# Expert weights split ahead of the loop and streamed from device memory, instead of split on chip in each sequence

## The chip, the cores and the metric

The kernel runs on one core of a Trainium2 chip. The core has five engines with queues of their own: TensorE (PE in the rows, its weight loads PEld), VectorE (DVE), ScalarE (ACT), GpSimd (POOL) and SyncE (SP), which here only issues DMAs. They meet through semaphores. The metric is the device time of one launch in microseconds (us). The kernel before takes 3360.27 us, the median of 3 runs (3360.13 to 3360.79).

## The reference

Two transformer-like layers over x of shape 8 x 1024 x 128 (8 sequences of 1024 tokens, width 128), all in float32. Both layers do `x = x + attention(layernorm(x)) + experts(layernorm(x))`:

```python
x  = h_t                                   # (8, 1024, 128)
xn = layernorm(x)
x  = x + latent_attention(xn) + experts_top2(xn)     # layer 0: 8 heads of 128, softmax over 1024 keys
xn = layernorm(x)
x  = x + linear_attention(xn) + experts_top4(xn)     # layer 1: 16 heads of 8, sums over tokens, no softmax matrix

# both mixtures: 8 experts, inner width 256, evaluated densely and weighted per token
for e in range(8):
    g, u = xn @ w_gate[e].T, xn @ w_up[e].T          # 128 -> 256 each
    out += weight[:, e:e+1] * (act(g, u) @ w_down[e].T)   # layer 0: silu(g)*u; layer 1: clipped, with biases
```

The router of layer 0 keeps two experts (thresholded softmax weights), that of layer 1 four.

## The kernel before

The program loops over the 8 sequences (`BATCH`, `SEQ = 1024`). All weights lie in SBUF from the start. Tokens lie as columns in the transposed tiles `xT[0]` and `xT[1]` (128 x 1024), one for each layer.

**Order of the work.** Nothing schedules this program: each engine's function is written out by hand, and each step waits on named semaphores. In layer 0 the attention has steps `w`, 0 to 71: 4 query projections, 32 score tiles (8 token blocks by 4 heads), again 4 queries and 32 tiles. A tile is: scores on PE, row maximum on DVE (L823), exponential on ACT (L551), transposes on PE two steps later (L1202), copied out half by ACT (L539) and half by DVE (L831), then the value product (L1216) for each four tiles. `UNIT_STEP` is 74; the last steps of the attention run beside the first expert units.

**Experts.** A layer has 16 chunks `f` (8 experts, two halves of 128 of the inner width) and 32 units `u` (a chunk by one half of the tokens). `gate_up(u)` makes six matmuls of 128x512 (L1121): each operand is split in a high part, rounded to the fast float32r format, and a low part, the rest, and the product is high x high + high x low + low x high, for gate and for up. In layer 0 ACT takes silu (L581) and DVE the product (L891); in layer 1 DVE adds the biases and clips (`limits`, L928 and L932), ACT takes silu (L604), DVE multiplies (L1037). POOL then multiplies by the routing weight (L450), and PE does `down(u)` four units later (L1128). `gate_up(u)` of layer 1 waits for `limits(u - 2)`, since the PSUM banks are two deep. Beside the units of layer 1, `flow_step(u)` does the linear attention in pieces (L951, L955, L977 and others on DVE; L1294, L1301, L1318 and L1326 on PE).

**Splits.** The high and low parts are made in each sequence. For the tokens, ACT casts `xT[l]` into `x_high` (L522) and DVE subtracts it for `x_low` (L802), in layer 0 at the end of the attention. For the weights ACT casts chunk `f` (128 x 256, L529) and DVE subtracts (L807), 16 chunks a layer, into one of four slots of `w_split`. `x_high`, `x_low` and `w_split` are views of `q_parts`, which holds the split queries of the attention, so none of them can be filled before the last score tiles have been read.

**Routing weights.** The transposed weights `gate_wT` go out to device memory (L390) and come back as one broadcast row of 512 KB for each expert (L398), in four slots. The first row of a layer is waited for by POOL.

**Before the loop.** SP issues the loads (L374 to L378). When all are in, ACT scales `w_down[1]` (L476), PE and DVE fold the attention's projections together (L634 and L636, L1053 to L1068), then the first sequence is normed.

Of the kernel before, what the change touches and what calls it, by code (L numbers as in the profile page):

```python
# [7 lines left out]
F32 = mybir.dt.float32  # L8
# [5 lines left out]
P = 128  # L14
# [28 lines left out]
ROUTER_EXP_STEPS = (18, 20)  # L43
GATES_STEP = QUAD + NT * QUAD + 3
# [46 lines left out]
UNITS_EACH = FH * HALVES  # L91

# [44 lines left out]
def two_layer_kernel(nc, ins, out):  # L137
    with ExitStack() as ctx:
# [69 lines left out]
        gate_rows = nc.dram_tensor("gate_rows", (2, E, SEQ), F32, kind="Internal").ap()  # L208
        ffn_s = sb("ffn_s", [P, 3, BANK])
# [27 lines left out]
        w_gate_up = [sb(f"w_gate_up{l}", [P, E * FH, 2, P]) for l in range(2)]  # L237
# [33 lines left out]
        def banks(a, n=2):  # L271
# [40 lines left out]
        w_high_ready = signal("w_high_ready", 2 * E * FH)  # L312
        w_low_ready = signal("w_low_ready", 2 * E * FH)
# [45 lines left out]
            (w_gate_up[0][:, :, :, :], "gate_up0"), (w_down[0][:, :, :], "down0"),  # L359
            (w_router[0][:, :], "router0"), (w_qkv[:, :], "W_QKV"), (w_proj[:, :], "W_PROJ"),  # L360
            (w_gate_up[1][:, :, :, :], "gate_up1"), (w_down[1][:, :, :], "down1"),
# [10 lines left out]
        def _(sp):  # L372
            for dst, name in loads:
                sp.dma_start(dst, ins[name]).then_inc(weights_in.sem, 16)  # L374
            for dst, name, n in rows:

                sp.dma_start(dst[:, 0:n], ins[name].partition_broadcast(P)).then_inc(weights_in.sem, 16)
            sp.dma_start(x_in[:, :, :], ins["x"][0, :, :].rearrange("(n p) d -> p n d", p=P)  # L378
                         ).then_inc(x_loaded.sem, 16)
            sp.sem_inc(y_stored.sem, 1)  # L380
            with sp.Fori(0, BATCH) as index:
# [5 lines left out]
                for l in range(2):  # L387
# [4 lines left out]
                    for e in range(E):  # L392
# [80 lines left out]
        def _(act):  # L473

            act.wait_ge(weights_in.sem, ALL_WEIGHTS)
# [30 lines left out]
            make_keys_high(None)  # L506
            with act.Fori(0, BATCH) as index:
# [7 lines left out]
                def split_high(l):  # L515

                    if l == 0:

                        act.wait_ge(scores_ready.sem, scores_ready.at(b, TILES - 2))
                    else:  # L520
                        act.wait_ge(xT_ready.sem, xT_ready.at(b, 2))
                    nc.scalar.copy(x_high, xT[l][:, :]).then_inc(x_high_ready.sem, 1)  # L522
# [906 lines left out]
```

## Time and profile before

| | |
|---|---|
| median of 3 runs | 3360.27 us |
| the profiled execution's own time | 3356.34 us |
| its span | 3354.5 us |
| granted TensorE clock, mean | 0.96 of full speed |
| PE busy | 3010.1 us, 90% of the span |
| DVE busy | 2371.5 us, 71% |
| ACT busy | 1556.0 us, 46% |
| POOL busy | 764.2 us, 23% |
| DMA | 89.17 MB, mean 27 GB/s |

The rows of the trace are from this one profiled execution. A busy share is a mean over stages: the sequence from about 462 to 872 us on the time axis is looked at below, because the first one contains the preparation. PE's shares flatter it, since the ends of matmuls are modelled; the waits stand more surely in the rows than the busy time does.

### The profile page before, as it was taken

What the parts mean: (1) busy time and instruction counts of PE and PEld (TensorE: products, weight loads), DVE (VectorE), ACT (ScalarE), POOL (GpSimd) and SP (SyncE); (2) the same over time, 40 slices, a digit from 0 to 9 for tenths busy, and PEclk for the clock granted to TensorE, in tenths of its full rate; (3) what the DMA queues carried; (4) which work ended last, traced back from release to release, by engine and by line L of the source; (5) the groups of instructions that cost most, each with busy time, mean ns of one, the idle gap of its engine ahead of it and who ended that gap; (6) DMA issues with size and microseconds to landing.
All of it is one profiled execution on the core that took longest, in us unless ns stands there. A gap on an engine that the chain in (4) does not pass through costs nothing.

```text
span 3354.5 us, 66466 instructions
## 1 busy us (share of the span) xinstructions
PE 3010.1 (90%) x21792; PEld 2176.3 (65%) x21792; DVE 2371.5 (71%) x3881; ACT 1556.0 (46%) x2742; POOL 764.2 (23%) x566
## 2 busy tenths in 40 slices
PE   5999889997899888998889988899788998999978
PEld 3786567765677556775567755677566775567755
DVE  3775777658776587765977659776597765977658
ACT  2663246623466234652356523565225652366423
POOL 0004320043201441013410235002340032500324
PEclk8999899999999899999999989999899998999989
DMA  2000100001000010000100001000000000000000
GB/s 103 11 23 26 51 15 27 7 21 51 14 27 8 19 51 14 27 14 13 51 15 27 21 13 45 15 27 21 32 26 14 27 27 32 20 15 27 26 32 26
DMA packets 40191, 89.17 MB, mean 27 GB/s; under 512 B 4048, under 2 KB 22681, under 8 KB 39321
## 3 DMA queue, kind: packets, MB, share of 16 engines
q1 hardware_dynamic: 39832, 84.55, 7.4%
q8 instruction: 206, 3.38, 0.4%
q14 instruction: 153, 1.25, 0.1%
HBM read 79.82 MB, written 4.72 MB: 25 GB/s over the span
## 4 chain that ended last, share of the span: by engine, by line
PE 69%; DVE 13%; issue 10%; ACT 4%; POOL 2%; DMA 1%; DVEq 1%; ACTq 0%; POOLq 0%; SPq 0%
PE ps L1121 16%; PE ps L1183 14%; PE ps L1202 12%; PE ps L1128 8%; PE ps L1216 7%; PE ps L1235 3%; DVE ffn_g L928 2%; DVE ffn_gu L1037 2%; DVE probsT L951 1%; PE ps L1093 1%; DVE ffn_u L932 1%; PE ps L1230 1%; PE ps L1294 1%; PE ps L1148 1%; ACT q_parts L512 1%
## 5 line engine op out<-in xcount | busy, mean ns | idle before, releaser
L450 POOL TENSOR_TENSOR probs<-ffn_gu,gate_bc 128x512 f32<-128x512 f32 x416 | 560.0, 1348 | 2331.4 <-DVE ffn_gu L891 1805.5
L1121 PE MATMUL ps<-q_parts 128*128 128x512 f32 x3072 | 940.4, 442 | 110.2 <-DVE ffn_u L932 58.0
L1121 PEld LDWEIGHTS ps<-q_parts 128*128 128x128 f32 x3072 | 569.2, 190 | 429.7 <-issue 230.9
L823 DVE TENSOR_REDUCE neg_max<-ps 128x1 f32<-128x1024 f32 x512 | 625.6, 1222 | 224.9 <-PE ps L1183 220.1
L551 ACT ACTIVATE probs<-ps,neg_max 128x1024 f32<-128x1024 f32 x512 | 571.3, 1116 | 223.5 <-DVE neg_max L823 220.6
L1183 PE MATMUL ps<-keys,q_parts 128*128 128x512 f32 x2048 | 606.9, 419 | 27.8 <-ACT probs L551 16.2
L1202 PE MATMUL ps<-ident,probs 128*128 128x128 f32 x4096 | 540.5, 274 | 18.1 <-DVE probsT L831 12.8
L1202 PEld LDWEIGHTS ps<-ident,probs 128*128 128x128 f32 x4096 | 478.8, 141 | 103.9 <-DVE probsT L831 21.7
L1128 PE MATMUL ps<-probs,w_down 128*128 128x512 f32 x832 | 436.8, 612 | 45.6 <-POOL probs L450 44.8
L1183 PEld LDWEIGHTS ps<-keys,q_parts 128*128 128x128 f32 x2048 | 347.7, 189 | 133.4 <-issue 64.3
L539 ACT COPY probsT<-ps 128x512 f32<-128x512 f32 x512 | 297.9, 582 | 203.8 <-PE ps L1202 203.4
L604 ACT ACTIVATE ffn_s<-ffn_g 128x512 f32<-128x512 f32 x256 | 160.7, 630 | 491.6 <-DVE ffn_g L928 491.4
L891 DVE TENSOR_TENSOR ffn_gu<-ffn_s,ps 128x512 f32<-128x512 f32 x256 | 175.4, 685 | 275.5 <-POOL probs L450 131.1
L831 DVE COPY probsT<-ps 128x512 f32<-128x512 f32 x512 | 348.3, 680 | 11.6 <-PE ps L1202 11.6
L581 ACT ACTIVATE ffn_s<-ps 128x512 f32<-128x512 f32 x256 | 152.9, 597 | 385.2 <-PE ps L1121 385.2
L1216 PE MATMUL ps<-probsT,latent 128*32 128x128 f32 x8192 | 276.7, 276 | 13.2 <-DVE x_mid L856 13.2
L1216 PEld LDWEIGHTS ps<-probsT,latent 128*32 128x32 f32 x8192 | 208.0, 109 | 57.6 <-DVE x_mid L856 23.8
L1128 PEld LDWEIGHTS ps<-probs,w_down 128*128 128x128 f32 x832 | 158.6, 193 | 112.3 <-POOL probs L450 69.0
L928 DVE TENSOR_SCALAR ffn_g<-ps,b_gate 128x512 f32<-128x512 f32 x256 | 190.0, 742 | 15.6 <-PE ps L1121 10.0
L816 DVE SCALAR_TENSOR_TENSOR q_parts<-ps,b_q,q_parts 128x1024 fp32r<-128x1024 f32 x64 | 82.1, 1283 | 126.7 <-ACT q_parts L512 126.7
L1037 DVE SCALAR_TENSOR_TENSOR ffn_gu<-ffn_u,ffn_s 128x512 f32<-128x512 f32 x176 | 138.1, 788 | 35.7 <-ACT ffn_s L604 35.7
L450 POOL TENSOR_TENSOR ffn_h<-ffn_gu,gate_bc 128x512 f32<-128x512 f32 x96 | 124.9, 1301 | 156.3 <-DVE ffn_gu L1037 114.4
(169 smaller groups left out, 2741.8 us busy)
## 6 DMA issues: line engine op xcount, KB each, us to landing
gate_bc<-gate_rows SPq DMA_DIRECT2D x128, 512.0 KB, 3.8
x_in<-in_x SPq DMA_DIRECT2D x9, 512.0 KB, 3.8
w_gate_up<-in_gate_up SPq DMA_DIRECT2D x2, 2048.0 KB
out<-x_mid SPq DMA_DIRECT2D x8, 512.0 KB, 3.4
w_down<-in_down SPq DMA_DIRECT2D x2, 1024.0 KB
probsT<-in_W_O SPq DMA_DIRECT2D x1, 512.0 KB
gate_rows<-gate_wT SPq DMA_DIRECT2D x16, 32.0 KB
w_qkv<-in_W_QKV SPq DMA_DIRECT2D x1, 192.0 KB
```

The costliest lines, as they stand in the source:

```text
L450: nc.gpsimd.tensor_tensor(ffn_h[u % 5], ffn_gu[:, u % 3, :], gate_bc[:, e % GATE_SLOTS, c * BANK:(c + 1) * BANK], ALU.mult).then_inc(h_rea ...
L539: nc.scalar.copy(probsT[:, t % (2 * QUAD), 0:BANK], ps[:, 4, :]).then_inc(low_copied.sem, 1)
L551: nc.scalar.activation(probs[:, t % 3, :], banks(2 * (t % 2)), ACT.Exp, bias=neg_max[:, t % 4:t % 4 + 1], accum_out=row_sum[:, g % 2, t % ...
L823: nc.vector.tensor_reduce(neg_max[:, t % 4:t % 4 + 1], banks(2 * (t % 2)), X, ALU.max, negate=True).then_inc(max_ready.sem, 1)
L831: nc.vector.tensor_copy(probsT[:, t % (2 * QUAD), BANK:SEQ], ps[:, 5, :]).then_inc(high_copied.sem, 1)
L928: nc.vector.tensor_scalar(ffn_g[:, u % 3, :], ps[:, u % 2, :], b_gate[:, f:f + 1], LIMIT, ALU.add, ALU.min).then_inc(gate_lim.sem, 1)
L1037: nc.vector.scalar_tensor_tensor(ffn_gu[:, u % 3, :], ffn_u[u % 3], 1.0 - LIMIT, ffn_s[:, u % 3, :], ALU.max, ALU.mult).then_inc(gu_done.s ...
L1121: mm = nc.tensor.matmul(ps[:, bank, :], w_split[:, f % 4, h, k * P:(k + 1) * P], tokens[:, half], start=(part == 0), stop=(part == 2))
L1128: nc.tensor.matmul(ps[:, 4 + c, :], w_down[l][:, f, :], ffn_h[u % 5], start=(l == 0 and f == 0), stop=(f == E * FH - 1)).then_inc(down_don ...
L1183: mm = nc.tensor.matmul(ps[:, 2 * (t % 2) + c, :], q_parts[:, j, part, n * P:(n + 1) * P], keys[:, c * BANK:(c + 1) * BANK], start=(part = ...
L1202: mm = nc.tensor.transpose(ps[:, 4 + c, i * P:(i + 1) * P], probs[:, t % 3, k * P:(k + 1) * P], ident[:, :])
L1216: nc.tensor.matmul(ps[DC * j:DC * (j + 1), 6 + g % 2, 0:P], latent[:, k, :], probsT[:, (g % 2) * QUAD + j, k * P:(k + 1) * P], start=(k == ...
```

## The change

The 16 chunks of each layer are split once before the loop. Both raw matrices (2 MB each) are loaded into room that is free at that time (`probsT` and the slots of `gate_bc`), ACT and DVE split them in four pieces of eight chunks through `q_parts`, and SP stores the parts in device memory (`w_parts`, 8 MB). In the loop, SP loads a chunk (high and low, 256 KB) into one of four slots as soon as `gate_up` has read the one before in that slot: 32 loads a sequence. The resident raw weights go. `x_high` and `x_low` get a buffer of their own, and those of layer 0 are made at step 30 of the attention.

```diff
+SPLIT_STEP = 30
+CHUNKS = E * FH
+CHUNK_SLOTS = 4
...
-        x_high, x_low = q_parts[:, 0, 0, :], q_parts[:, 0, 1, :]
-        w_split = q_parts[:, 1, :, :].rearrange("p a b -> p (a b)").rearrange("p (s h c) -> p s h c", s=4, h=2)
+        x_parts = sb("x_parts", [P, 2, SEQ], F32R)
+        x_high, x_low = x_parts[:, 0, :], x_parts[:, 1, :]
+        w_split = sb("w_split", [P, CHUNK_SLOTS, 2, 2 * P], F32R)
+        w_parts = nc.dram_tensor("w_parts", (2 * CHUNKS, P, CHUNK), F32, kind="Internal").ap()
+        w_prep = q_parts[:, :, :, :].rearrange("p a b c -> p (a b c)").rearrange("p (s f h c) -> p s f h c", s=2, h=2, c=2 * P)
...
@@ block.sync
+            sp.dma_start(x_in[:, :, :], ins["x"][0, :, :].rearrange("(n p) d -> p n d", p=P)
+                         ).then_inc(x_loaded.sem, 16)
+            for l in range(2):
+                sp.dma_start(w_raw[l], ins[f"gate_up{l}"].rearrange("p f a b -> p f (a b)")).then_inc(raw_in[l].sem, 16)
             for dst, name in loads:
...
+            for i in range(4):
+                sp.wait_ge(prep_low.sem, i + 1)
+                sp.dma_start(w_parts[8 * i:8 * i + 8, :, :].rearrange("f p c -> p f c"),
+                             w_prep[:, i % 2, :, :, :].rearrange("p f h c -> p f (h c)").bitcast(F32)
+                             ).then_inc(parts_stored[i % 2].sem, 16)
...
+                    for e in range(GATE_SLOTS):
+                        load_row(e)
+                    for f in range(CHUNK_SLOTS, CHUNKS + CHUNK_SLOTS):
+                        if f % FH == 0 and GATE_SLOTS <= f // FH < E:
+                            load_row(f // FH)
+                        w = l * CHUNKS + f
+                        sp.wait_ge(gu_ready.sem, gu_ready.at(b, (w - CHUNK_SLOTS + 1) * HALVES))
+                        load_chunk(w)
@@ block.scalar
+            for i in range(4):
+                if i % 2 == 0:
+                    act.wait_ge(raw_in[i // 2].sem, 16)
+                if i >= 2:
+                    act.wait_ge(parts_stored[i % 2].sem, 16)
+                nc.scalar.copy(w_prep[:, i % 2, :, 0, :], w_raw[i // 2][:, 8 * (i % 2):8 * (i % 2) + 8, :]
+                               ).then_inc(prep_high.sem, 1)
...
-                    if w == STEPS - 1:
+                    if w == SPLIT_STEP:
                         split_high(0)
-                        split_weights_high(0, 0)
-                    if w == STEPS:
-                        split_weights_high(0, 1)
...
@@ block.vector
+            for i in range(4):
+                dve.wait_ge(prep_high.sem, i + 1)
+                nc.vector.tensor_tensor(w_prep[:, i % 2, :, 1, :], w_raw[i // 2][:, 8 * (i % 2):8 * (i % 2) + 8, :],
+                                        w_prep[:, i % 2, :, 0, :].bitcast(F32), ALU.subtract
+                                        ).then_inc(prep_low.sem, 1)
...
-                    if w == STEPS:
+                    if w == SPLIT_STEP + 1:
                         split_low(0)
-                    if w == STEPS + 1:
-                        split_weights_low(0, 0)
-                        split_weights_low(0, 1)
...
-                    if u % HALVES == 1 and f + 3 < E * FH:
-                        split_weights_low(1, f + 3)
@@ block.tensor
-                        pe.wait_ge(w_low_ready.sem, w_low_ready.at(b, l * E * FH + f + 1))
+                        w = l * CHUNKS + f
+                        pe.wait_ge(w_loaded[w % CHUNK_SLOTS].sem, w_loaded[w % CHUNK_SLOTS].at(b, 16 * (w // CHUNK_SLOTS + 1)))
```

Each of the other calls of `split_weights_high` and `split_weights_low` goes as well. The line numbers in the pieces of order below are those of the kernel that the sentence names.

DVE in layer 1, beside the linear attention, before (`ISA` rows are waits or semaphore steps; `ffn_g`, `ffn_u` and `ffn_gu` are an expert unit's tiles, `inv_flow` is the linear attention's):

```order
L1037 SCALAR_TENSOR_TENSOR ffn_gu<-ffn_u,ffn_s 128x512
L955 TENSOR_REDUCE inv_flow<-probsT 128x128
L656 ISA
L806 ISA
L807 TENSOR_TENSOR q_parts<-w_gate_up,q_parts 128x256
L925 ISA
L927 ISA
L928 TENSOR_SCALAR ffn_g<-ps,b_gate 128x512
```

and now:

```order
L1060 SCALAR_TENSOR_TENSOR ffn_gu<-ffn_u,ffn_s 128x512
L980 TENSOR_REDUCE inv_flow<-probsT 128x128
L693 ISA
L951 ISA
L953 ISA
L954 TENSOR_SCALAR ffn_g<-ps,b_gate 128x512
```

The subtraction of the weights and its wait are gone from between the reduction and the next unit's bias and clip.

ACT at the end of layer 0's attention, before (L551 is the last exponential, L539 the copies of transposed probabilities):

```order
L551 ACTIVATE probs,row_sum<-ps,neg_max 128x1024
L519 ISA
L522 CAST q_parts<-xT 128x1024
L529 CAST q_parts<-w_gate_up 128x256
L537 ISA
L538 ISA
L539 COPY probsT<-ps 128x512
L529 CAST q_parts<-w_gate_up 128x256
```

and now:

```order
L594 ACTIVATE probs,row_sum<-ps,neg_max 128x1024
L580 ISA
L581 ISA
L582 COPY probsT<-ps 128x512
L580 ISA
L581 ISA
L582 COPY probsT<-ps 128x512
```

The token cast now stands at step 30, between a scale copy and a copy of transposed probabilities:

```order
L607 COPY out_room<-ps 128x128
L573 CAST x_parts<-xT 128x1024
L580 ISA
L581 ISA
L582 COPY probsT<-ps 128x512
```

SP in layer 1, from the routing weights' way out to the first rows behind them, before:

```order
L390 DMA gate_rows<-gate_wT 8x1024
L391 ISA
L397 ISA
L398 DMA gate_bc<-gate_rows 128x1024
L397 ISA
L398 DMA gate_bc<-gate_rows 128x1024
L397 ISA
L398 DMA gate_bc<-gate_rows 128x1024
L397 ISA
L398 DMA gate_bc<-gate_rows 128x1024
L395 ISA
L398 DMA gate_bc<-gate_rows 128x1024
```

and now, from the fourth row on:

```order
L430 DMA gate_bc<-gate_rows 128x1024
L440 ISA
L407 DMA w_split<-w_parts 128x512
L440 ISA
L407 DMA w_split<-w_parts 128x512
L440 ISA
L407 DMA w_split<-w_parts 128x512
L440 ISA
L407 DMA w_split<-w_parts 128x512
L427 ISA
L430 DMA gate_bc<-gate_rows 128x1024
```

Four chunk loads, each behind its own wait, now stand between the fourth and the fifth row.

## Rows read from the trace of the kernel before

A timeline row reads: start us, busy us, engine, line, operation, out<-in, shapes, count, and in brackets the idle time before it with its releaser. A row of the stages reads: stretch, its length, then PE, PEld, DVE, ACT and POOL busy with counts, the granted clock, the DMA share and GB/s.

**Rows 1.** Busy time by stage: layer 0's experts, layer 1's first part, its last part.

```profile
656.70:729.90 73.20, 72.95 (x327) 49.54 (x328) 38.65 (x78) 24.32 (x50) 41.72 (x33) 1.00 0.08 30
774.40:838.40 64.00, 56.74 (x211) 37.99 (x212) 59.42 (x82) 18.59 (x35) 30.97 (x21) 0.95 0.12 46
838.40:872.20 33.80, 31.69 (x134) 20.85 (x133) 27.95 (x42) 9.31 (x17) 18.35 (x14) 1.00 0.00 1
```

**Rows 2.** Groups by line, weight and token splits: busy us, mean ns | idle before.

```profile
L807 DVE TENSOR_TENSOR q_parts<-w_gate_up,q_parts 128x256 fp32r<-128x256 f32 x256 | 147.5, 581 | 4.2
L802 DVE TENSOR_TENSOR q_parts<-xT,q_parts 128x1024 fp32r<-128x1024 f32 x16 | 19.5, 1221 | 0.7
L522 ACT CAST q_parts<-xT 128x1024 fp32r<-128x1024 f32 x16 | 16.6, 1039 | 0.3
```

**Rows 3.** L807 alone in layer 1's DVE stretch: stretch, length, DVE busy, clock, DMA.

```profile
780.00:838.40 58.40, 5.32 (x8) 0.97 0.10 37
```

**Rows 4.** Timeline of PE in layer 1, where it waits for DVE.

```profile
798.46 1.65 PE L1121 MATMUL ps<-q_parts 128*128 128x512 f32 x6 [1.32 <-DVE ffn_u L932]
810.33 1.65 PE L1121 MATMUL ps<-q_parts 128*128 128x512 f32 x6 [0.55 <-DVE ffn_u L932]
818.16 2.68 PE L1121 MATMUL ps<-q_parts 128*128 128x512 f32 x6 [2.02 <-DVE out_room L932]
836.78 1.65 PE L1121 MATMUL ps<-q_parts 128*128 128x512 f32 x6 [0.71 <-DVE out_room L932]
```

**Rows 5.** Timelines of DVE and POOL in layer 1: a short split, a long one.

```profile
792.72 0.47 DVE L807 TENSOR_TENSOR q_parts<-w_gate_up,q_parts 128x256 fp32r<-128x256 f32 x1
799.52 2.10 POOL L450 TENSOR_TENSOR probs<-ffn_gu,gate_bc 128x512 f32<-128x512 f32 x1 [0.71 <-DVE ffn_gu L1037]
800.42 1.48 DVE L807 TENSOR_TENSOR q_parts<-w_gate_up,q_parts 128x256 fp32r<-128x256 f32 x1
```

**Rows 6.** Timeline, from the attention to layer 0's experts.

```profile
654.29 1.09 PE L1202 MATMUL ps<-ident,probs 128*128 128x128 f32 x8 [0.26 <-ACT probsT L539]
655.42 0.69 DVE L831 COPY probsT<-ps 128x512 f32<-128x512 f32 x1 [0.72 <-PE ps L1202]
656.70 1.66 PE L1121 MATMUL ps<-q_parts 128*128 128x512 f32 x6 [1.31 <-DVE q_parts L807]
```

**Rows 7.** Timeline, steps 32 to 35 of the attention.

```profile
551.14 1.11 ACT L551 ACTIVATE probs<-ps,neg_max 128x1024 f32<-128x1024 f32 x1 [1.06 <-DVE neg_max L823]
552.90 1.23 DVE L823 TENSOR_REDUCE neg_max<-ps 128x1 f32<-128x1024 f32 x1 [0.66 <-PE ps L1183]
553.49 1.17 PE L1183 MATMUL ps<-keys,q_parts 128*128 128x512 f32 x4
557.71 1.23 DVE L823 TENSOR_REDUCE neg_max<-ps 128x1 f32<-128x1024 f32 x1 [0.93 <-PE ps L1183]
```

**Rows 8.** Before the loop: a stage while the loads run, then the timeline.

```profile
10.00:15.00 5.00, 0.00 (x0) 0.00 (x0) 0.00 (x0) 0.00 (x0) 0.00 (x0) 1.00 0.98 415
27.43 1.91 ACT L476 ACTIVATE w_down<-w_down 128x2048 f32<-128x2048 f32 x1 [25.34 <-DMA b_router<-in_b_ROUTER]
28.68 0.18 DVE L634 TENSOR_SCALAR probsT<-ps 33x32 f32<-33x32 f32 x1 [28.68 <-PE ps L1053]
31.64 0.17 DVE L636 TENSOR_SCALAR probsT<-probsT 33x32 f32<-33x32 f32 x1
33.23 2.01 PE L1066 MATMUL ps<-probsT 33*128 33x1 f32 x16
```

**Rows 9.** DMA issues of the page: count, KB each, us to landing.

```profile
gate_bc<-gate_rows SPq DMA_DIRECT2D x128, 512.0 KB, 3.8
out<-x_mid SPq DMA_DIRECT2D x8, 512.0 KB, 3.4
```

**Rows 10.** Timeline of SP and PE in layer 1: rows issued, and chunk 4's unit.

```profile
769.10 57.90 SPq L398 DMA_DIRECT2D gate_bc<-gate_rows  x8
787.62 1.65 PE L1121 MATMUL ps<-q_parts 128*128 128x512 f32 x6 [0.36 <-DVE ffn_u L932]
```

More of the change, by code:

```diff
@@ L91 @@
 UNITS_EACH = FH * HALVES
+CHUNKS = E * FH
+CHUNK_SLOTS = 4
+CHUNK = 2 * 2 * P
 def step_of(t):
@@ L208, in two_layer_kernel @@
         gate_rows = nc.dram_tensor("gate_rows", (2, E, SEQ), F32, kind="Internal").ap()
+        w_raw = [v.rearrange("p (f c) -> p f c", c=2 * P)
+                 for v in (room[:, 4 * SEQ:8 * SEQ], gate_bc[:, :, :].rearrange("p s c -> p (s c)"))]
         ffn_s = sb("ffn_s", [P, 3, BANK])
@@ L311, in two_layer_kernel @@
         x_low_ready = signal("x_low_ready", 2)
-        w_high_ready = signal("w_high_ready", 2 * E * FH)
-        w_low_ready = signal("w_low_ready", 2 * E * FH)
+        raw_in = [signal(f"raw_in{l}") for l in range(2)]
+        prep_high = signal("prep_high")
+        prep_low = signal("prep_low")
+        parts_stored = [signal(f"parts_stored{i}") for i in range(2)]
+        w_loaded = [signal(f"w_loaded{i}", 2 * CHUNKS // CHUNK_SLOTS * 16) for i in range(CHUNK_SLOTS)]
         logits_mm = signal("logits_mm", 2)
@@ L377, in _, with load_chunk @@
                 sp.dma_start(dst[:, 0:n], ins[name].partition_broadcast(P)).then_inc(weights_in.sem, 16)
-            sp.dma_start(x_in[:, :, :], ins["x"][0, :, :].rearrange("(n p) d -> p n d", p=P)
-                         ).then_inc(x_loaded.sem, 16)
             sp.sem_inc(y_stored.sem, 1)
+            for i in range(4):
[3 more added lines that the diff above has]
+                             ).then_inc(parts_stored[i % 2].sem, 16)
+            for i in range(2):
+                sp.wait_ge(parts_stored[i].sem, 32)
+            def load_chunk(w):
+                w %= 2 * CHUNKS
+                sp.dma_start(w_split[:, w % CHUNK_SLOTS, :, :].rearrange("p h c -> p (h c)").bitcast(F32), w_parts[w, :, :]
+                             ).then_inc(w_loaded[w % CHUNK_SLOTS].sem, 16)
+            for w in range(CHUNK_SLOTS):
+                load_chunk(w)
             with sp.Fori(0, BATCH) as index:
@@ L391, in _, with load_row @@
                     sp.wait_ge(rows_stored.sem, rows_stored.at(b, 16 * (l + 1)))
-                    for e in range(E):
+                    def load_row(e):
                         if e >= GATE_SLOTS:
@@ L506, in _ @@
             make_keys_high(None)
+            for i in range(2):
+                act.wait_ge(parts_stored[i].sem, 32)
             with act.Fori(0, BATCH) as index:
@@ L515, in split_high @@
                 def split_high(l):
-                    if l == 0:
-                        act.wait_ge(scores_ready.sem, scores_ready.at(b, TILES - 2))
-                    else:
+                    if l == 1:
                         act.wait_ge(xT_ready.sem, xT_ready.at(b, 2))
+                        act.wait_ge(gu_ready.sem, gu_ready.at(b, UNITS))
                     nc.scalar.copy(x_high, xT[l][:, :]).then_inc(x_high_ready.sem, 1)
-                def split_weights_high(l, f):
-                    if l == 1 or f >= 4:
-                        act.wait_ge(gu_ready.sem, gu_ready.at(b, l * UNITS + (f - 3) * HALVES))
-                    nc.scalar.copy(w_split[:, f % 4, 0, :], w_gate_up[l][:, f, :, :].rearrange("p a b -> p (a b)")
-                                   ).then_inc(w_high_ready.sem, 1)
                 def attention_step(w):
@@ L597, in _ @@
                 for u in range(UNITS):
-                    if u % HALVES == 0 and u // HALVES + 3 < E * FH:
-                        split_weights_high(1, u // HALVES + 3)
                     act.wait_ge(gate_lim.sem, gate_lim.at(b, u + 1))
@@ L692, in _ @@
             assert count[0] == DVE_STEPS_BEFORE, count[0]
+            for i in range(2):
+                dve.wait_ge(parts_stored[i].sem, 32)
             with dve.Fori(0, BATCH) as index:
```

22 lines of the change are left out of this document (3 added, 19 removed).

## Prediction

> **What bounds the kernel now.** I read the busy shares of the page first, then the chain of waits, then the stages of one sequence, and last the timelines at the places that the change touches. PE is busy for nine tenths of the span, so the reader has to see where PE is not the one that decides. In layer 0's experts it is: 72.95 of 73.20 us busy, with DVE at 38.65. In layer 1's first part (774.4 to 838.4) DVE decides: 59.42 of 64.0 us busy, and PE leaves 7.3 us open. In its last part PE is at 31.69 of 33.8 again [rows 1]. The PE timeline says the same: in the first part `gate_up` starts when DVE's clip of two units earlier ends [rows 4].
>
> **What goes from the loop, and what it is worth.** The weight splits on DVE are 256 of 581 ns, 147.5 us in all [rows 2]. That is not the gain. Half of them stand in layer 0, beside work that PE bounds. I cost those at nothing: PE's 72.95 us cover them. ACT's casts go at the same places, and ACT waits for DVE or PE there; nothing for them either.
>
> Term 1, layer 1. In 780 to 838.4 eight subtractions take 5.32 us [rows 3]. Most are like the one at 792.72, under half a microsecond; one at 800.42 takes 1.48 [rows 5]. What DVE saves reaches the end only where PE waited for it. Up to 798.46 DVE has lost two of the short ones, about 1.0 us with the gaps between instructions, and PE, which waited for DVE there, comes 1.0 earlier. Then PE runs without a wait to the one of 0.55 at 810.33, and can gain that; then 2.02 at 818.16 and 0.71 at 836.78 [rows 4]. Sum 1.0 + 0.55 + 2.02 + 0.71 = 4.3 us, less than the 5.3 that DVE saves, so PE's waits set it. After 838.4 PE is solid and the gain is only carried on. Bounds: 0, if each saved microsecond comes back as a wait of DVE for PE, and 7.3, all that PE left open.
>
> Term 2, the start of layer 0's experts. `gate_up(0)` waits 1.31 us, at last for the first weight subtraction, and starts at 656.70. The last transposes before it start 0.26 late because ACT is at the token cast; DVE's copy of them (655.42, 0.69) then ends 0.26 earlier, at 655.85, and nothing else is waited for [rows 6]. 656.70 - 655.85 = 0.85; I take 0.8. Bounds: 0 and 1.57, the wait and the 0.26.
>
> Term 3, the token split at steps 30 and 31. It puts 1.04 us on ACT and 1.22 on DVE [rows 2] in the middle of the attention. DVE's maximum of step 32 comes 1.2 later, so ACT's exponential (551.14, 1.11) ends at about 553.5, just when the scores of step 34 began (553.49). Before the queries DVE waits for PE 0.66 and 0.93 [rows 7], 1.59 together, and that takes up the 1.22. I take a loss of 0.2 for the slips at the edges; bounds 0 and 2.3, both in series.
>
> Between the layers two subtractions go from DVE ahead of its adding of the experts' result. PE has to finish the last `down` products and four to eight transposes before that, so I take nothing; at most it is 2 x 0.58 us a sequence [rows 2]. Each sequence: 4.3 + 0.8 - 0.2 = 4.9 us, eight times 39.
>
> **What is added.** The 32 chunk loads of a sequence are issued by SP, whose other work is rows and waits. The nearest DMA is a row of 512 KB, 3.8 us to landing [rows 9]; a chunk of half that size has some 13 us in layer 0 (three chunks at two units each, 73.20 us for 32 units [rows 1]). The tightest is chunk 4 of layer 1, behind four rows issued from 769.10 on; its unit starts at 787.62 [rows 10]. Four rows at 415 GB/s [rows 8] are 5 us, the chunk less than one, so it lands before 780. Cost nothing. Behind SP's new waits stand rows 4 to 7 of a layer; each waits for a unit that is far behind the one the chunk waits for, and its slot is used eight units later, 18 us in layer 0. The eviction to device memory and the rows of the first experts are not behind any new wait.
>
> **Before the loop.** This is serial and paid once. The loads run at 415 GB/s, and the last one is in at 27.43; DVE starts folding at 28.68 and ends at 31.81, PE goes on at 33.23, so 1.4 us of a DVE delay are free [rows 8]. The first sequence's x and the raw matrices come first now, 4.5 MB or 11 us at that rate, so pieces 0 and 1 are split while the other loads still run. SP has the loads to issue first, and the stores queue behind them: 2 MB at 415 GB/s are 5.1 us; 512 KB out of `x_mid` landed in 3.4 [rows 9], of which 1.3 is data at that rate and 2.1 the way. Store 0 is done at 27.4 + 5.1 + 2.1 = 34.6, store 1 at 39.7. Piece 3 may be cast then: ACT takes 1.91 for 128x2048 [rows 8], DVE 2 x 1.22 [rows 2], end at 44.0. Shift 44.0 - 28.68 = 15.3, less 1.4: 14 us. The stores of pieces 2 and 3 run beside the folding, and the wait for them ahead of the loop ends by about 51, before the first sequence is normed (53 + 14). Bounds: 7 if the first store gets through some 7 us sooner, ahead of the last loads, and 29 if each store takes four times 3.4.
>
> **The sum.** 3356.3 (the profiled execution) - 39 + 14 = 3331; the median of the runs lies 3.9 above the profiled one, so 3335.
>
> **A rule to weigh.** The subtraction at 800.42 took 1.48 us, while POOL's product ran from 799.52 to 801.62; the one at 792.72, with POOL at rest, took 0.47 [rows 5]. The Trainium skill, "SBUF — State Buffer" on the shared port pair, says that DVE and GpSimd exclude each other for a whole instruction when DVE reads two SBUF inputs. With this rule the trace agrees. It speaks against a full gain: a wait like that goes to whichever two-input instruction of DVE meets POOL, and taking the subtraction away may only hand it on. As a mechanism of this kernel that is rival (a), priced from rows.
>
> **Rivals.** (a) The collisions are handed on. POOL's products stay, and L1037 and the linear attention's products also read two tiles from SBUF. Two long subtractions in the stretch are worth about 1.9 us more than short ones (5.32 against 8 x 0.42); then DVE saves 3.4, PE perhaps 3.0: 8 x (3.0 + 0.6) = 29, 3342 + 4 = 3345. Against: the next instruction after each is a bias from PSUM. 0.2. (b) More: the matmuls at 818.16 took 2.68 against 1.65 after the wait of 2.02, and the granted clock of the stretch is 0.95 [rows 1, 4]. So part of that stretch ran at 1.2 instead of 2.4 GHz, right after PE had stood still; if the wait goes, the extra 1.0 goes too: 8 us more, 3327. 0.15. (c) PE takes over in layer 1 as in its last part, where it is solid while DVE is at 27.95 of 33.8 [rows 1]. Then term 1 is 0, the loop gives 8 x 0.6 = 5, and the preparation costs 14: 3369, slower. It decides when term 1 is below (14 - 5) / 8 = 1.1 us. Against it stand the waits for DVE in rows 4. 0.1. (d) Stores are slow, 13.6 us each: preparation 29, 3350. 0.07. (e) A chunk comes late: SP stands in a wait for a row while a slot is free. It needs more than 13 us in layer 0 or 8 in layer 1; at 1 us for a late chunk and two a sequence it costs 16, 3351; from four a sequence on (25 / 8 = 3.1) the kernel is slower. 0.03. The forecast itself has 0.45.
>
> **How the numbers follow.** 3335. Its own range is 3325 to 3345. The cases (a), (b) and (d) lie within 3317 and 3358, with DVE's full 5.3 and a preparation of 10 at the low end (3356.3 - 8 x 5.9 + 10 + 3.9 = 3323, 6 more for the clock), and part of (c) at the high one. I give 3317 to 3358. A difference under 0.2%, 7 us, can't be told from none. Faster by more: the forecast, (a), (b), (d) and some of the rest, 0.82; the same 0.07; slower 0.11.
>
> **What would show it.** Right: in layer 1's first part DVE's busy time falls by 5 us or more and the stage by about 4; `gate_up(0)` of layer 0 is released by a copy (L831's counterpart) and not by a split; PE never waits for `w_split`'s DMA; the loop starts near 67 instead of 53. Wrong: the first part keeps its length and DVE shows waits for PE in it; PE rows with a DMA of `w_split` as releaser; a start of the loop beyond 80; a stretch of the attention around step 32 longer by more than 0.5.

## The result, and the profile after

The changed kernel takes 3334.24 us (median of 6 runs, 3324.31 to 3341.4), the one before 3360.53 beside it (6 runs, 3351.23 to 3364.9): ratio 0.9921, 95% interval 0.99 to 0.9943. The forecast was 3335 us, faster. The profiled execution took 3329.43 us, against 3356.34 before; the prediction's sum for it was 3331.

The page of the changed kernel, busy time with the share of the span, DMA, the chain of waits, and two DMA issues (count, KB each, us to landing):

```profile
span 3327.7 us, 66006 instructions
PE 3000.2 (90%) x21792; PEld 2170.9 (65%) x21792; DVE 2257.9 (68%) x3629; ACT 1486.0 (45%) x2490; POOL 757.3 (23%) x566
DMA packets 81783, 165.66 MB, mean 50 GB/s; under 512 B 8272, under 2 KB 26905, under 8 KB 80921
PE 70%; DVE 12%; issue 10%; ACT 3%; POOL 1%; DMA 1%; DVEq 1%; POOLq 0%; ACTq 0%; SPq 0%
w_split<-w_parts SPq DMA_DIRECT2D x260, 256.0 KB, 2.6
w_parts<-q_parts SPq DMA_DIRECT2D x4, 2048.0 KB, 8.9
```

DVE has 113.6 us less (2371.5 before), ACT 70, PE 10. DMA has nearly twice the bytes, and only 1% of the chain. So 114 us off DVE became 27 off the span.

Where they went shows when each sequence is cut at the same instructions in both traces. Means over the 8 sequences, in us, with the prediction's figure for a sequence:

| stretch, from to | before | after | x 8 | predicted |
|---|---|---|---|---|
| before the loop, to the first `x_in` issue of the loop | 82.4 | 94.5 | +12.1 | +14 once |
| `x_in` issue to the store of `gate_rows`, layer 0 (most of the attention) | 81.42 | 81.46 | +0.3 | +0.2 |
| that store to the first `gate_up` of layer 0 | 79.01 | 78.31 | -5.6 | -0.8 |
| layer 0's experts, to the transposes after them | 76.43 | 76.51 | +0.6 | 0 |
| transposes to layer 1's `gate_rows` store | 34.57 | 34.86 | +2.3 | 0 |
| that store to the output store | 106.28 | 102.04 | -33.9 | -4.3 |
| output store to the next sequence's `x_in` issue (7 times) | 35.14 | 34.72 | -2.9 | 0 |

The sum is -27.1, against -26.9 between the profiled executions, so nothing is left over.

**Layer 1.** Its stretch in the second sequence, cut at four points: the store of `gate_rows`, the second sums matmul, the first output matmul of the linear attention, and the output store. First before, then after; the columns are those of [rows 1]:

```profile
766.01:800.81 34.80, 26.26 (x84) 16.25 (x85) 27.76 (x37) 10.93 (x18) 14.81 (x10) 0.90 0.27 92
800.81:839.13 38.32, 34.78 (x140) 23.70 (x139) 37.03 (x54) 14.36 (x26) 17.75 (x13) 0.96 0.08 28
839.13:872.22 33.09, 30.98 (x132) 20.60 (x131) 27.22 (x41) 8.76 (x15) 18.04 (x13) 1.00 0.00 1
```

```profile
770.10:804.00 33.90, 26.75 (x85) 16.59 (x85) 25.78 (x32) 9.15 (x12) 14.68 (x10) 0.90 0.37 118
804.00:839.01 35.01, 32.93 (x139) 22.91 (x138) 33.13 (x48) 12.68 (x20) 17.70 (x13) 1.00 0.26 91
839.01:872.11 33.10, 30.98 (x132) 20.59 (x131) 26.54 (x38) 8.47 (x14) 17.99 (x13) 1.00 0.15 41
```

0.90 us are gained in the first stretch, 3.31 in the second, nothing in the third, where PE has 31 of 33.1 busy in both. The second is the one with DVE at 37.03 of 38.32, and DVE has 3.90 less there. PE's timeline after, where [rows 4] has waits of 1.32, 0.55, 2.02 and 0.71:

```profile
801.66 1.64 PE L1145 MATMUL ps<-x_parts,w_split 128*128 128x512 f32 x6 [1.32 <-DVE ffn_u L958]
815.86 1.63 PE L1145 MATMUL ps<-x_parts,w_split 128*128 128x512 f32 x6
818.64 1.64 PE L1145 MATMUL ps<-x_parts,w_split 128*128 128x512 f32 x6 [0.28 <-DVE out_room L958]
822.41 1.64 PE L1145 MATMUL ps<-x_parts,w_split 128*128 128x512 f32 x6 [1.27 <-DVE ffn_u L958]
836.67 1.64 PE L1145 MATMUL ps<-x_parts,w_split 128*128 128x512 f32 x6
```

DVE is still what PE waits for; the wait of 2.02 is now 0.28, the one of 0.71 gone, but a unit later there is a new one of 1.27. And the matmuls that took 2.68 take 1.64. PE, at 32.93 of 35.01, is now busy nearly as long as DVE, at 33.13.

**The start of layer 0's experts.** It answers to [rows 6]; there the releaser of the last row was the weight subtraction L807, after 1.31 us:

```profile
658.34 1.09 PE L1226 MATMUL ps<-ident,probs 128*128 128x128 f32 x8
659.47 0.69 DVE L864 COPY probsT<-ps 128x512 f32<-128x512 f32 x1 [1.70 <-PE ps L1226]
660.39 1.65 PE L1145 MATMUL ps<-x_parts,w_split 128*128 128x512 f32 x6 [0.96 <-DVE probsT L864]
```

The copy sets it now, and the transposes (658.34) no longer wait for ACT.

**Before the loop.** ACT, DVE and PE, answering to [rows 8]:

```profile
9.58 3.70 ACT L523 CAST q_parts<-probsT 128x2048 fp32r<-128x2048 f32 x2 [7.48 <-DMA probsT<-in_gate_up]
30.50 1.90 ACT L523 CAST q_parts<-gate_bc 128x2048 fp32r<-128x2048 f32 x1 [17.23 <-DMA w_parts<-q_parts]
35.55 1.90 ACT L523 CAST q_parts<-gate_bc 128x2048 fp32r<-128x2048 f32 x1 [3.15 <-DMA w_parts<-q_parts]
37.48 2.29 DVE L664 TENSOR_TENSOR q_parts<-gate_bc,q_parts 128x2048 fp32r<-128x2048 f32 x1 [2.75 <-ACT q_parts L523]
52.14 0.29 DVE L700 BATCH_NORM_STATS2 stats<-x_in 128x6 f32<-128x128 f32 x1
```

Two pieces are split while the loads run. The third stands 17.23 us for its slot, whose content is on its way to device memory; the first norm starts at 52.14 (39.34 before).

PE's folding pays a second time. These are its last two groups and the clock while they run; before, the first of them was at 33.23 with 2.01 [rows 8], and the second is the last line:

```profile
42.87 3.57 PE L1089 MATMUL ps<-probsT 33*128 33x1 f32 x16 [11.65 <-DVE probsT L673]
46.37 3.78 PE L1091 MATMUL ps<-probsT 32*128 32x512 f32 x4
42.87:50.15 7.28, 7.28 (x20) 4.65 (x20) 0.00 (x0) 0.00 (x0) 0.00 (x0) 0.50 0.75 272
```

```profile
35.16 2.19 PE L1068 MATMUL ps<-probsT 32*128 32x512 f32 x4
```

After its wait of 11.65 us for DVE, PE has half the clock (0.50, which is 1.2 GHz of 2.4), and the two groups take 7.28 us, where they took 4.12.

### The profile page after: what moved, and what is told of

Its sections match the earlier page's. It is cut to its first block, busy times and chain, and to the rows that moved or that the text cites. A ratio compares the mean times of both kernels' runs of the same rounds, so it can differ in the third digit from the quotient of the medians.

```text
span 3327.7 us, 66006 instructions
## 1 busy us (share of the span) xinstructions
PE 3000.2 (90%) x21792; PEld 2170.9 (65%) x21792; DVE 2257.9 (68%) x3629; ACT 1486.0 (45%) x2490; POOL 757.3 (23%) x566
## 4 chain that ended last, share of the span: by engine, by line
PE 70%; DVE 12%; issue 10%; ACT 3%; POOL 1%; DMA 1%; DVEq 1%; POOLq 0%; ACTq 0%; SPq 0%
PE ps L1145 16%; PE ps L1207 14%; PE ps L1226 12%; PE ps L1152 9%; PE ps L1240 7%; PE ps L1259 3%; DVE ffn_u L958 1%; DVE probsT L864 1%; DVE probsT L976 1%; PE ps L1116 1%; DVE ffn_gu L1060 1%; PE ps L1172 1%; PE ps L1318 1%; PE ps L1254 1%; ACT q_parts L565 1%
## 5 line engine op out<-in xcount | busy, mean ns | idle before, releaser
L1145 PE MATMUL ps<-x_parts,w_split 128*128 128x512 f32 x3072 | 940.8, 442 | 89.7 <-DVE ffn_u L958 60.2
L1145 PEld LDWEIGHTS ps<-x_parts,w_split 128*128 128x128 f32 x3072 | 567.6, 189 | 402.1 <-issue 223.0
L1226 PE MATMUL ps<-ident,probs 128*128 128x128 f32 x4096 | 541.0, 273 | 16.8 <-DVE probsT L864 12.8
L1060 DVE SCALAR_TENSOR_TENSOR ffn_gu<-ffn_u,ffn_s 128x512 f32<-128x512 f32 x176 | 140.1, 800 | 38.0 <-ACT ffn_s L636 38.0
```

Of the source, the lines that this page charges most:

```text
L1145: mm = nc.tensor.matmul(ps[:, bank, :], w_split[:, f % 4, h, k * P:(k + 1) * P], tokens[:, half], start=(part == 0), stop=(part == 2))
L1226: mm = nc.tensor.transpose(ps[:, 4 + c, i * P:(i + 1) * P], probs[:, t % 3, k * P:(k + 1) * P], ident[:, :])
```

## The experiments

All runs here are 5 rounds, each beside the kernel before on the same chip. Intervals are 95%. Line numbers differ by a few from kernel to kernel.

**Put the subtractions of layer 1 back, as dead work.** Each writes a tile that nothing reads and waits for the one before; 13 a sequence at the old places.

```diff
                     if u % HALVES == 1 and f + 3 < CHUNKS:
+                        nc.vector.tensor_tensor(burn[:, 0, :], w_q[:, 0:2, :]..., w_q[:, 2:4, :]..., ALU.subtract)
```

> The changed kernel with 13 subtractions of 128x256 (two SBUF inputs, result not used) put back on VectorE at the old places in layer 1's expert loop, each behind a wait on the one before. Theory (VectorE decides layer 1's first part, and PE's waits there set the gain of 4.3 us a sequence): the 4.2 us of that stretch come back, 8 x 4.2 = 34 us, so about 3368, and the other stages keep their length. Rival 1 (the gain came from something else in the change, such as the buffers of their own): under 8 us, below 3342. Rival 2 (each microsecond of VectorE counts): 13 x 0.58 x 8 = 60 us, 3394.

Measured: 3370.66 us (3364.08 to 3379.15), ratio to before 1.0036 (1.0022 to 1.0049), so 36 more than the changed kernel. From layer 1's store to the output store it takes 106.31 us a sequence, against 106.28 before and 102.04 after: the whole gain of layer 1 is this. Its second stretch, cut as above, and in it two of the subtractions with the POOL product that one of them meets:

```profile
818.87:857.22 38.35, 35.01 (x140) 23.54 (x139) 37.06 (x54) 12.57 (x20) 17.75 (x13) 0.96 0.26 83
826.52 0.42 DVE L1060 TENSOR_TENSOR burn<-w_q 128x256 fp32r<-128x256 f32 x1
832.40 2.09 POOL L495 TENSOR_TENSOR probs<-ffn_gu,gate_bc 128x512 f32<-128x512 f32 x1 [2.08 <-DVE ffn_gu L1067]
833.50 1.27 DVE L1060 TENSOR_TENSOR burn<-w_q 128x256 fp32r<-128x256 f32 x1
836.23 2.10 PE L1152 MATMUL ps<-x_parts,w_split 128*128 128x512 f32 x6 [2.00 <-DVE out_room L962]
```

Of the 104 subtractions 17 are long, 9 of 1.48 and 8 of 1.27 us, about one of each in a sequence; the others take 0.41 to 0.47. Each long one began while a POOL product ran and ends 0.28 or 0.29 us after that product does (834.77 and 834.49 in the rows), whenever it began: it waits for POOL. PE's wait of 2.00 is back. The 104 are 60 us of DVE's busy time (578 ns in the mean), and cost 36.

**The same number of reads, one input, from PSUM.** Twelve a sequence, in the same units' `limits`:

```diff
+                    if u % HALVES == 0 and 4 <= u <= 26:
+                        nc.vector.tensor_scalar(burn[:, 0, :], ps[:, 2 + u % 2, 0:2 * P], 1.0, None, ALU.add)
```

> As the first, but the 12 added VectorE instructions read one tile of 128x256 from PSUM instead of two from SBUF, so they last about the same when GpSimd is at rest. Theory A (collisions with GpSimd were part of the old cost, two a sequence of about 1 us each): less than for the first, by up to 2 us a sequence, so 3345 to 3358 where the first is 3368. Theory B (PE's waits set the size, the collisions are swallowed): 3362 to 3368, the same as the first within 7.

Measured: 3353.35 us (3337.33 to 3367.11), ratio 0.9966 (0.9944 to 0.9987): 19 over the changed kernel, where the subtractions cost 36. The view of the tile (count, min/median/max in ns) and the second stretch:

```profile
L964 DVE TENSOR_SCALAR burn<-ps x96: 405/410/416, 372.0 to 3331.0; 128x256 fp32r<-128x256 f32 x96
810.88:847.49 36.61, 33.08 (x139) 22.83 (x138) 35.11 (x54) 12.68 (x20) 17.70 (x13) 1.00 0.26 87
```

None of them is over 416 ns, though 64 of the 96 ran beside a POOL product. DVE's busy time is 1.95 less than with subtractions, and the two collisions are (1.48 - 0.42) + (1.27 - 0.42) = 1.91; the stretch is 1.74 shorter. So the two meetings with POOL were not time that would be spent anyway: by these two kernels they are 1.74 of the 3.34 us that the subtractions add to the second stretch, and over the whole of layer 1 1.66 (106.31 less 104.65) of 4.27 (106.31 less 102.04). (One of the 13 and the exact places differ, which I can't separate from this.)

**Casts of the weights on ACT in layer 1**, 13 a sequence, and **both halves of the splits in layer 0**, 14 on each engine:

```diff
+                    if u % HALVES == 0 and u // HALVES + 3 < CHUNKS:      # layer 1, ACT
+                        nc.scalar.copy(burn[:, 2, :], w_q[:, 0:2, :]...)
```

```diff
+                    if u % HALVES == 0 and u // HALVES + 2 < CHUNKS:      # layer 0, ACT
+                        nc.scalar.copy(burn[:, 2, :], w_q[:, 0:2, :]...)
+                    if u % HALVES == 1 and u // HALVES + 2 < CHUNKS:      # layer 0, DVE
+                        nc.vector.tensor_tensor(burn[:, 0, :], w_q[:, 0:2, :]..., w_q[:, 2:4, :]..., ALU.subtract)
```

> The changed kernel with 13 casts of 128x256 (result not used) put back on ScalarE in layer 1's expert loop. Theory (ScalarE waits for VectorE's clip there, the casts cost nothing): 3334 within 7. Rival (ScalarE's silu is on the chain after its table loads, and a cast ahead of it is too): 0.4 to 1 us a sequence, 3 to 8 us more.

> The changed kernel with 14 subtractions of 128x256 on VectorE and 14 casts of 128x256 on ScalarE (results not used) put back at the old places in layer 0's expert loop. Theory (PE is the bound there and covers them): no difference, 3334 within 7. Rival (engine time counts wherever it is): 14 x 0.58 x 8 = 65 us, 3399.

Measured: casts in layer 1 3337.88 us (3331.31 to 3341.74), ratio 0.9923 (0.9905 to 0.9941); both in layer 0 3339.11 us (3334.53 to 3345.19), ratio 0.9936 (0.9919 to 0.9953). Neither is told from the changed kernel. In the trace of the first, layer 1 takes 102.85 us in the mean, 0.8 more than in the changed kernel. But its second stretch is 35.01 as there; two sequences of about 105 make the mean, both longer in the first stretch, and such a sequence comes without casts too (103.49 with the late token split below, 104.29 with the preparation in place). So no cost is shown. In the trace of the second, layer 0's experts take 76.50 us, against 76.51: 112 subtractions and 112 casts, of the 256 each that the change removed from the loop, are worth nothing there. 16 of those subtractions met POOL and took 1.40 to 1.41 us, which cost nothing either.

**No stream.** Only the first four chunks are loaded, once, and used for all; the weights of the other 28 of 32 are left out.

```diff
-                        sp.wait_ge(gu_ready.sem, gu_ready.at(b, (w - CHUNK_SLOTS + 1) * HALVES))
-                        load_chunk(w)
...
-                        pe.wait_ge(w_loaded[w % CHUNK_SLOTS].sem, w_loaded[w % CHUNK_SLOTS].at(b, 16 * (w // CHUNK_SLOTS + 1)))
+                        pe.wait_ge(w_loaded[w % CHUNK_SLOTS].sem, 16)
```

> The changed kernel without the chunk loads in the loop: only the first four chunks are loaded, once, and every chunk of both layers uses one of these slots, so 28 of 32 chunks' weights are left out. Theory (the loads are hidden and disturb nothing): 3334 within 7. Rival (64 MB more through the DMA engines slow the rows of routing weights, the fetch of instructions or the engines' SBUF accesses): faster by over 7, 3327 or less.

Measured: 3332.25 us (3328.52 to 3335.56), ratio 0.9924 (0.9911 to 0.9937). 67 MB less to read change nothing that can be measured; the stretches of the table are within 0.1 us, but for the one before the loop (94.24, 0.3 less) and two that move from sequence to sequence in every kernel, the one between the layers (last section) and the one after the output store (33.9 to 36.5 us).

**Two slots, and two slots in another order.** The first shrinks `CHUNK_SLOTS` from 4 to 2. The second does too, but issues chunk 2 of layer 1 ahead of the wait for the routing weights:

```diff
-CHUNK_SLOTS = 4
+CHUNK_SLOTS = 2
...
-                            mm = nc.tensor.matmul(ps[:, bank, :], w_split[:, f % 4, h, k * P:(k + 1) * P],
+                            mm = nc.tensor.matmul(ps[:, bank, :], w_split[:, f % CHUNK_SLOTS, h, k * P:(k + 1) * P],
```

```diff
                 for l in range(2):
+                    if l == 1:
+                        sp.wait_ge(gu_ready.sem, gu_ready.at(b, (CHUNKS + 1) * HALVES))
+                        load_chunk(CHUNKS + 2)
                     sp.wait_ge(gateT_ready.sem, gateT_ready.at(b, l + 1))
...
+                        if w == CHUNKS + 2:
+                            continue
```

> The changed kernel with two chunk slots instead of four. In layer 0 a chunk is then loaded while the other is used, 4.5 us, and a load lands 2.6 us after issue in the trace (7.1 at most, behind rows): theory: no wait in layer 0 beyond the few loads behind a row; in layer 1 chunk 2 is loaded only behind the four rows, near 778 on the axis of the kernel before, where its unit stands at 766 and the next units at 780: about 8 us of a wait, part of it inside PE's wait for the first row, so 2 to 5 us a sequence; 3350 to 3375. Rival (landing time hides completely also here): 3334 within 7. Rival (every chunk waits 1 us or more): 8 x 32 = 250 us more.

> Two slots for chunks again, but SP issues chunk 2 of layer 1 ahead of the return of the routing weights instead of behind the four broadcast rows. With two slots in the plain order PE waited 11.5 to 12.0 us for that chunk once in each sequence, and the kernel took 73 us more than the changed one. Theory A (the order in SP's queue makes the wait, not the number of slots): the wait for the chunk is gone, all others have been covered, and the time is that of the changed kernel with four slots, 3334 us, or up to 8 more if chunk 3, which stays behind the rows, comes late by up to 1 us: 3330 to 3345. Theory B (two slots are too few in layer 1 while rows are on the way): the wait moves to chunk 3, two units later, and most of the 73 us stays, 3380 or more.

Measured: 3407.62 us (3400.32 to 3420.7), ratio 1.0159 (1.0138 to 1.018), 73 over the changed kernel and more than I had expected; then 3337.47 (3321.77 to 3340.84), ratio 0.9915 (0.9894 to 0.9935). The first one's trace, SP and PE in layer 1 (the routing weights stored at 777.05):

```profile
778.92 1.28 SPq L430 DMA_DIRECT2D gate_bc<-gate_rows  x3
780.80 26.36 SPq L407 DMA_DIRECT2D w_split<-w_parts  x4
787.46 2.93 PE L1145 MATMUL ps<-x_parts,w_split 128*128 128x512 f32 x6 [11.47 <-DMA w_split<-w_parts]
```

The wait comes 8 times in the trace, 11.47 to 11.98 us, and no unit waits for a chunk elsewhere, not in layer 0 either. It is unit 4, whose chunk SP can only issue after it has waited for the routing weights to arrive in device memory and come back in rows; the chunk then lands behind them, some 6.7 us after its issue. With the chunk first no wait for one is left, and the stretch from the store to the sums is 9.46 us instead of 18.53 (9.41 in the changed kernel). So the order in SP's queue makes this wait, and four slots hide it: with them the first chunk behind the rows is chunk 4, used at 791.10, four units after. This is rival (e) made to happen. What I missed for two slots is that the whole turn of the routing weights stands ahead of that chunk, not only the four rows.

**Token parts last**, at the steps of the kernel before:

```diff
-SPLIT_STEP = 30
+SPLIT_STEP = STEPS - 1
```

> The changed kernel with the token split of layer 0 back at the end of the attention (steps 71 and 72 instead of 30 and 31). Theory (terms 2 and 3): the start of layer 0's experts comes later by 0.3 to 0.7 us a sequence, since ScalarE's cast delays the copy ahead of the last transposes again and VectorE's subtraction stands ahead of its copy; the attention's middle gains 0.05. Net 2 to 5 us: 3336 to 3339, in the trace 78.6 to 79.0 us from the first layer's routing weights to the first expert unit against 78.3 now. Rival (the gain of 0.7 came from the missing weight subtractions alone): 78.3 as now.

Measured: 3332.07 us (3330.72 to 3337.07), ratio 0.9921 (0.9908 to 0.9934), not told from the changed kernel. The trace tells more. `gate_up(0)` of layer 0 still starts 78.33 us after the store (78.31; 79.01 before), where I had expected 78.6 to 79.0, so term 2 is all weight split and nothing of it is the tokens'. The stretch of the attention is 81.10, against 81.46: splitting them at step 30 costs 0.36. Here is where, PE's transposes of that step in the changed kernel and, at the same place, with the late split:

```profile
558.54 1.37 PE L1226 MATMUL ps<-ident,probs 128*128 128x128 f32 x8
559.84 1.08 PE L1240 MATMUL ps<-probsT,latent 128*32 128x128 f32 x32
```

```profile
562.27 1.03 PE L1226 MATMUL ps<-ident,probs 128*128 128x128 f32 x8
563.24 1.08 PE L1240 MATMUL ps<-probsT,latent 128*32 128x128 f32 x32
```

**Preparation in place.** The high part gets a piece of `q_parts` of its own for each of the four pieces, and the low part overwrites the raw weights; nothing waits for a store before it can be split. Each piece is stored by two DMAs, the high parts and the low.

```diff
+        w_high = q_parts[:, :, :, :].rearrange("p a b c -> p (a b c)").rearrange("p (i f c) -> p i f c", i=4, c=2 * P)
...
-                if i >= 2:
-                    act.wait_ge(parts_stored[i % 2].sem, 16)
-                nc.scalar.copy(w_prep[:, i % 2, :, 0, :], w_raw[i // 2]...)
+                nc.scalar.copy(w_high[:, i, :, :], w_raw[i // 2]...)
...
+                raw = w_raw[i // 2][:, 8 * (i % 2):8 * (i % 2) + 8, :]
+                nc.vector.tensor_tensor(raw.bitcast(F32R), raw, w_high[:, i, :, :].bitcast(F32), ALU.subtract)
```

> The changed kernel with the preparation made without a turnaround: all high parts of the 32 chunks fit into the room for the split queries, the low parts are written over the raw weights, so ScalarE and VectorE don't wait for a store; each piece is stored by two DMAs with runs of 1 KB. Theory (the preparation costs 12.8 us because pieces 2 and 3 wait for the stores): all splits end near 21 us, before the other loads are in; the loop starts about 13 us sooner, 3334 - 13 = 3321. Rival (the stores themselves, 8 MB, are what the loop waits for): the runs of 1 KB make them slower than 20 us, the first query waits for them until 60 or later, and the time stays at 3330 or above.

Measured: 3321.47 us (3305.07 to 3326.36), ratio 0.9877 (0.9858 to 0.9897), 13 less than the changed kernel. From its timeline:

```profile
16.26 4.49 DVE L662 TENSOR_TENSOR gate_bc<-gate_bc,q_parts 128x2048 fp32r<-128x2048 f32 x2 [0.45 <-ACT q_parts L520]
37.73 0.29 DVE L697 BATCH_NORM_STATS2 stats<-x_in 128x6 f32<-128x128 f32 x1
47.23 2.19 SPq L407 DMA_DIRECT2D w_split<-w_parts  x4
```

All four pieces are split by 20.8, while the loads are still on their way, and the first norm starts at 37.73 instead of 52.14. PE no longer waits for DVE in its folding, and the two groups that took 7.28 us take 1.94 and 2.65. The stores run beside it; the first chunks are issued at 47.23, as late as in the changed kernel (47.24), and it harms nothing.

**Both together**, in place and the tokens late:

> The preparation in place, and the token parts split after the last score tiles (steps 71 and 72) as in the kernel before. In the trace of the kernel with only the late split the stretch of the attention is 0.36 us shorter in each sequence (81.10 against 81.46) and the start of layer 0's experts is not later (78.33 both), so eight times 0.36 is 3 us: 3321.5 less 3, 3318.5. Theory A (the two changes add): 3313 to 3323, with the stretch at 81.1 and the first norm at about 37.7 us. Theory B (the 0.36 is given back by a wait elsewhere, or was a matter of one trace): 3321.5, not told from the kernel in place. The times spread by some 10 us, so the two are told by the stretches of the trace rather than by the median.

Measured: 3316.3 us (median of 5 runs, from 3307.89; one of the five took 7182 us at a full granted clock, which no trace explains), ratio 0.9868 (0.9848 to 0.9888). The stretch of the attention is 81.12, the first norm starts at 37.80: the two add, as far as 5 us can be told. It is the fastest version, 47 us under the 3363.22 of the kernel before beside it.

## Why the prediction was right, step by step

**Term 1, layer 1: 4.3, measured 4.24.** The place and the size were right: 0.94 up to the second sums matmul (1.0 predicted), 3.32 from there to the linear attention's output (0.55 + 2.02 + 0.71 = 3.28), both means over 8 sequences. How it was counted was only half right. I took the gain to be PE's waits going. They did not all go. In the second stretch PE's idle time fell from 38.32 - 34.78 = 3.54 to 35.01 - 32.93 = 2.08, by 1.46; the other 1.85 is PE's busy time, and that is the clock, 0.96 before and 1.00 after. The same stretch in four kernels says what really sets its length:

| kernel | length | DVE busy | PE busy | PE idle | clock |
|---|---|---|---|---|---|
| before | 38.32 | 37.03 | 34.78 | 3.54 | 0.96 |
| 13 subtractions back | 38.35 | 37.06 | 35.01 | 3.34 | 0.96 |
| 12 PSUM reads | 36.61 | 35.11 | 33.08 | 3.53 | 1.00 |
| changed | 35.01 | 33.13 | 32.93 | 2.08 | 1.00 |

In all four the length is DVE's busy time plus 1.3 to 1.9, whatever PE does with the rest: it waits, or it is busy for longer at the lower clock. DVE's 3.90 less became 3.31, and 0.6 went into new waits of DVE. So that 3.28 met 3.32 was in part luck: the waits gave less than half of it. Nor does the load taken off DVE give the size as it stands. Of each microsecond that DVE had more or less in this table, the length had 0.81 to 0.89: 3.31 of 3.90 for the change, 3.34 of 3.93 with the subtractions back, 1.60 of 1.98 with the PSUM reads, 1.74 of 1.95 between the last two. The table is of the second sequence; the means over eight are within 0.15 of it.

The 0.94 is less sure. The first stretch moves from sequence to sequence, and in the traces of the versions that have nothing put back in layer 1 and four slots its mean is 33.87 to 34.27, against 34.86 before and 33.93 in the changed kernel.

**Term 2, 0.8, measured 0.70.** Released by the copy as predicted; late tokens show that the weight split alone held it.

**Term 3, a loss of 0.2, measured 0.36 by the late split.** Between before and after it shows as 0.04, because about 0.3 came back a little earlier: PE's wait of 0.25 for DVE's scaling of the value product (L848) at 550.02 in the kernel before is not in the traces of either version of the changed kernel, at the same place. What took it away I did not look for.

**Beside PE, nothing: right.** The splits that run beside layer 0's units are worth nothing, 14 of its 16 chunks, and no worth of layer 1's casts can be shown. Nothing was gained between the layers either: 34.57 to 34.86 is the clock (below).

**The stream, nothing: right.** No row of PE has a DMA of `w_split` as releaser; 67 MB less change nothing.

**Before the loop, 14, measured 12.8** from norm to norm, 12.1 to the loop's first issue, a stretch that lies between 94.07 and 97.49 in the traces of the kernels with this preparation. The size came out by two errors that nearly cancel. The estimate had the first slot free at 34.6; it was at 30.50, and the second at 35.55 (39.7 estimated). The store is issued at 19.99, so it did not wait for the last load to be in (25.66), as I had it; the splits ended at 39.77, 4.2 before the 44.0 of the sum. Against that the sum has no clock in it: PE went on at 42.87 instead of 33.23, 9.6 later, and then took 7.28 instead of 4.12 for the same two groups, 3.2 more. 9.6 and 3.2 are the 12.8.

The prediction also puts the first norm at 53; it stands at 39.34 in the trace before. Nothing in its sum rests on that.

**The rivals.** (a) Collisions handed on: DVE's products (L1037, now L1060) are the two-input instructions that could inherit them. Their groups, before and after, count, busy us, mean ns:

```profile
L1037 DVE SCALAR_TENSOR_TENSOR ffn_gu<-ffn_u,ffn_s 128x512 f32<-128x512 f32 x176 | 138.1, 788 | 35.7 <-ACT ffn_s L604 35.7
L1037 DVE SCALAR_TENSOR_TENSOR ffn_gu<-out_room,ffn_s 128x512 f32<-128x512 f32 x80 | 78.2, 977 | 0.0
```

```profile
L1060 DVE SCALAR_TENSOR_TENSOR ffn_gu<-ffn_u,ffn_s 128x512 f32<-128x512 f32 x176 | 140.1, 800 | 38.0 <-ACT ffn_s L636 38.0
L1060 DVE SCALAR_TENSOR_TENSOR ffn_gu<-out_room,ffn_s 128x512 f32<-128x512 f32 x80 | 79.0, 988 | 0.0
```

They grew by 2.8 us in all, 0.35 a sequence, of the 1.91 that went, while the linear attention's own products of 128x1024 lost 1.1 in all. So if it happens it is for a fifth at most, and it does not decide. Which instructions can meet is seen in the two experiments: 17 of 104 subtractions of two SBUF tiles were long, none of the 96 reads from PSUM was. The rule cited in the prediction (the Trainium skill, "SBUF — State Buffer", "Who interferes with whom") says too that a DVE instruction with at most one SBUF input does not contend with GpSimd, outside the two-port modes. With both halves these counts agree.

(b) A clock bonus on top: the mechanism is there, the bonus is not. In the kernel before, the stretch of 2 us that holds the wait of 2.02 and the two after it:

```profile
816.00:818.00 2.00, 0.14 (x1) 0.00 (x0) 2.00 (x4) 0.52 (x1) 0.42 (x1) 1.00 0.00 0
818.00:820.00 2.00, 1.84 (x5) 1.49 (x6) 1.97 (x4) 0.11 (x1) 1.21 (x1) 0.61 0.00 0
820.00:822.00 2.00, 2.00 (x5) 0.86 (x4) 1.97 (x5) 1.47 (x2) 0.07 (x1) 0.53 0.00 0
```

PE stands still, then the granted clock falls to near 1.2 of the 2.4 GHz. After the change all such stretches between 816 and 826 have 1.00. But DVE is full in all three rows, so the faster PE only waits for it sooner: the new 1.27 at 822.41. (c) PE takes over: refuted, term 1 is 4.24 and not 0, and with the subtractions back DVE costs the same again. (d) Slow stores: the two that ACT stood for took 10.4 and 14.7 us from issue, but overlapped, and were in at 30.4 and 35.5; so no. (e) A late chunk: not with four slots; with two it costs 9 us a sequence.

## What to carry to other kernels

Work on an engine that is full in one stage and idle in others is worth what it is in that stage alone: of 114 us taken from DVE, the splits beside layer 0's units gave nothing and about 34 us came from one stretch of some 73 in each sequence. Count there the busy time of the full engine, its waits for POOL included, as the most that can come back (here 0.81 to 0.89 of it did); the waits of the other engine are no sure measure, for here 1.46 of their 3.54 went and the rest of the gain came as a higher clock. A wait of PE ahead of serial work is paid twice, as itself and in the clock after it (11.65 us, then 3.2 more). A stream through a queue that also carries a round trip needs enough slots to last for that round trip (here two were too few and four enough), or the first chunk ahead of it. And a one-time preparation should be checked for slots that wait for a store, which was 13 us here, a third of what the loop gained.

## What had not been expected

The stretch between the layers (router of layer 1 to its `gate_rows` store) has the same instructions in each sequence and does not take the same time. Three sequences of the changed kernel, the columns as in [rows 1]:

```profile
746.40:770.10 23.70, 18.29 (x64) 12.13 (x64) 13.71 (x27) 3.62 (x5) 0.00 (x0) 0.83 0.00 0
1152.10:1179.06 26.96, 22.26 (x66) 14.44 (x67) 13.71 (x27) 3.62 (x5) 0.00 (x0) 0.72 0.00 0
2380.25:2405.65 25.40, 20.25 (x64) 13.14 (x64) 13.71 (x27) 3.61 (x5) 0.00 (x0) 0.75 0.00 0
```

It comes in three lengths, 23.7, 25.4 and 26.95, with a granted clock of 0.83, 0.75 and 0.72, and DVE and ACT busy for the same time in all. In the kernel before it alternates strictly between 23.35 and 26.57 to 26.84. The mean is 25.05 there and 25.35 here, which is the +2.3 of the table; eight sequences at one length or another make up to 26 us, as wide as the spread of the runs of one kernel. Why one sequence gets the one and the next the other is open. It also means that edits of 3 us have to be read in the stretches of the trace, as with the late tokens, and not in medians.
